# Latent attention on one core: values in three runs of 2, 4 and 4 units in place of five of 2, with a ring of ten places for probabilities

## Chip, core and metric

The kernel runs on one core of a Trainium2 chip. The metric is device time of the whole launch in microseconds (us). Engines: PE is TensorE (PEld its weight loads), DVE is VectorE, ACT is ScalarE, POOL is GpSimd, SP is SyncE.

## What is computed

The input is 4 sequences of 1024 tokens with 128 channels. Six residual blocks follow one another: a mixture of experts, an attention with a polynomial in place of softmax, the mixture again, a feed-forward block, the latent attention, and the feed-forward block again. Only the latent attention (`attn1_phase`) is touched:

```python
Wdkv = x @ latent_w + latent_b                     # keys = values, 36 wide
q = einsum('btc,hcl->bhtl', x, Wd_w) + Wd_b        # 16 heads
scores = einsum('bhtl,bsl->bhts', q, Wdkv) / sqrt(8)
attn = softmax(where(causal, scores, -inf))
y = einsum('bhts,bsl->bhtl', attn, Wdkv)
out = y.transpose(0, 2, 1, 3).reshape(b, t, 576) @ out_w + out_b
```

## The kernel before

The order of the work is written out by hand, per engine, with semaphores. The latent attention goes through 4 sequences ("elements") of 8 pairs of heads. For a pair `m` two things go on at once: its own exponentials and values, and the row maxima of pair `m + 1`, which have to be known before the scores of that pair can be exponentiated.

**Units.** The causal scores of a pair, keys on the partitions, are cut into 10 units (`NU`, L1734). Units 0 to 6 belong to the queries 512 to 1023, units 7 to 9 to the queries 0 to 511. Units 0 to 2 and 7 to 9 lie on the diagonal; POOL zeroes the forbidden part of their probabilities (L1886). Each unit exists for both heads (c = 0, 1). `scores` (L1974) writes one unit and head into one of three PSUM banks; it waits for the exponential three places back (L1972). ACT takes the exponential (L2174) into `probs`, a ring of `RING` = 4 units in SBUF, and waits for the values of the unit `RING` places back (L2172). `values` (L1990) multiplies the two heads' probabilities with V, the heads beside each other in two 64-column halves of the array; every float32 product is two matmul records, and a run of two full units has 8 records, one with a split unit 12. Unit 2 and unit 9 are half as wide (256 columns).

**Maxima.** `scores_max` (L1959) computes the scores of 16 query tiles of the next pair again, queries on the partitions, and DVE reduces each to its row maximum (L2277) and writes it with a short read of its accumulator. Wide tiles (5 to 8 key tiles, 640 to 1024 columns) share one place of two PSUM banks; narrow ones (128 to 512 columns) share a third bank. Each kind has only one buffer: the matmuls of a wide tile wait for DVE to be through with the wide tile before (L1956), and so with the narrow ones. The 16 tiles are dealt into 8 slots, called M0 to M7 here: M0 is one wide tile, M3 is narrow, wide, narrow, and the others are wide, narrow.

**Order on PE** (`pair`, L2012 to L2065), five steps `d` for a pair; S is the scores of one unit and head, V a unit's values:

- d = 0: S 0, S 0, S 1, M0, S 1, then V 8 and V 9 of the pair before
- d = 1: M1, S 2, S 2, S 3, M2, S 3, then V 0, V 1
- d = 2: M3, S 4, S 4, S 5, M4, S 5, then V 2, V 3
- d = 3: M5, S 6, S 6, S 7, M6, S 7, then V 4, V 5
- d = 4: M7, S 8, S 8, S 9, S 9, the transpose of the maxima (L1965), the query projection of pair m + 3 (L1943), then V 6, V 7

The last pair of an element does V 8 and V 9 at its own end. In pair 6 of the first three elements (the opening pair) the latents of the next element are computed in d = 0, and V 8, V 9 and a projection stand ahead of M0, so M0 and M1 follow each other with nothing between. At the start of a pair the first S waits for the maxima to come by DMA into the rows of `qS` (L1971); SP issues those (L1822, L1824) after ACT and DVE have split the transposed maxima in two parts. ACT copies the finished sums out of PSUM (`copy_out`, L2162), the first half after V 6, the second after V 9.

Of the kernel before, what the change touches and what calls it, by code (L numbers as in the profile page):

```python
# [34 lines left out]
def after(n):  # L35

    return n + 1 + LEAD
# [1633 lines left out]
def attn1_phase(nc, t, tag):  # L1671


    with ExitStack() as ctx:
        def sb(name, shape, dt=F32):
            return ctx.enter_context(nc.sbuf_tensor(f"{tag}_{name}", shape, dt))
# [23 lines left out]
        ml = sb("ml", [16, 2, P], F32R)  # L1700
        probs = sb("probs", [P, RING, 2, HALF])
        yT = sb("yT", [P, PAIRS, SEQ])
# [62 lines left out]

        def ring(q, u):

            return (u + 2 * q) % RING

        def o_part(j, rows, n):  # L1770

# [33 lines left out]
        def follows(i, k, more):  # L1805

            return more or i + k < PAIRS

        def projected(i, more):

            return (more or i + 3 < PAIRS) and i != OPENS

        with nc.Block() as block:
# [97 lines left out]
            def _(pe):  # L1911
# [4 lines left out]
                def transpose_x(b):  # L1916
                    for s in range(2):
                        pe.wait_ge(xn_ready, after(b * BT + 4 * s + 3))
                        for j in range(4):
                            last = pe.transpose(m_bank[s][:, j * P:(j + 1) * P], xn[:, 4 * s + j, :], t.ident)  # L1920
                        last.then_inc(xt_ready, 1)

                def latents(b):
                    for s in range(2):
                        pe.wait_ge(xl_ready, after(b * 2 + s))
                        for k, (a, w) in enumerate(PRODUCTS):
                            last = pe.matmul(m_bank[s][0:STACK, :], lat[w][:, :], xT[a][:, s * HALF:(s + 1) * HALF],
                                             start=k == 0, stop=k == 2)
                        last.then_inc(kp_ready, 1)

                def latent_rows(b):
                    pe.wait_ge(xl_ready, after(b * 2 + 1))
                    for j in range(BT):
                        for k, (a, w) in enumerate(PRODUCTS):
                            last = pe.matmul(m_bank[2][:, j * VW:j * VW + LAT], xT[a][:, j * P:(j + 1) * P], lat[w][:, 0:LAT],
                                             start=k == 0, stop=k == 2)
                    last.then_inc(vp_ready, 1)

                def project(p, i):
                    for h, s in enumerate(HALVES):  # L1940
                        pe.wait_ge(qs_ready, after((p - 1) * 2 + h))
                        for k, (a, w) in enumerate(PRODUCTS):
                            last = pe.matmul(m_bank[h][0:2 * LAT, :], wd[w][:, i * 2 * LAT:(i + 1) * 2 * LAT],  # L1943
                                             xT[a][:, s * HALF:(s + 1) * HALF], start=k == 0, stop=k == 2)
                        last.then_inc(qp_ready, 1)

                def scores_max(m, q, n, keys, spare=False):
                    c, j = IN_ORDER[n]
                    before = bank_before(n, spare)
                    if not of_kind(n) and j >= 4:  # L1950
                        pe.wait_ge(q_in[q][0], (m - q) * 48 + 96)
                    elif not of_kind(n):
                        pe.wait_ge(q_in[q][1], (m - q) * 24 + 48)
                        pe.wait_ge(q_first[q], (m - q) * 24 + 48)
                    if before >= 0:
                        pe.wait_ge(mx_ready, after(m * 16 + before))  # L1956
                    for lo in range(0, (j + 1) * P, HALF):
                        hi = min(lo + HALF, (j + 1) * P)
                        last = pe.matmul(max_part(n, lo, hi, spare), qS[q][0:STACK, c, j * P:(j + 1) * P], keys[0:STACK, lo:hi],  # L1959
                                         start=True, stop=True)  # L1960
                    last.then_inc(sm_ready, 1)

                def transpose_max(m, q):
                    pe.wait_ge(mx_ready, after(m * 16 + 15))
                    pe.transpose(o_part(0, 16, P), mx[:, q, :], t.ident).then_inc(mt_ready, 1)  # L1965

                def scores(m, q, u, c):
                    s, pieces = units[u]
                    k = 2 * u + c
                    if u == 0 and c == 0:  # L1970
                        pe.wait_ge(m_in, (m + 1) * 32)  # L1971
                    pe.wait_ge(p_ready, after(m * NE + k - 3 if k >= 3 else (m - 1) * NE + (18, 19, 17)[k]))  # L1972
                    for kt, at_, qc, n, _ in pieces:
                        last = pe.matmul(e_part(k, at_, at_ + n), kS[:, kt * P:(kt + 1) * P],  # L1974
                                         qS[q][:, c, s * HALF + qc:s * HALF + qc + n], start=True, stop=True)
                    last.then_inc(s_ready, 1)
# [35 lines left out]
                def pair(m, i, b, more):  # L2012
                    q = i % 2
                    ahead = follows(i, 1, more)
                    opening = more and i == OPENS + 1
                    keys = kN if i == PAIRS - 1 else kS

                    def maximum(k):
                        if not ahead:
                            return  # L2020
                        if k == 0:
                            if follows(i, 2, more):
                                pe.wait_ge(qs_ready, after((m + 2) * 2 + 1))
                            pe.wait_ge(ml_ready, after(m))
                            if opening:
                                pe.wait_ge(v_ready, after(b + 1))
                        if k == 1 and i == 0:
                            pe.wait_ge(res.xo_ready, after(b * BT - 1))
                        for n in range(FIRST[k], FIRST[k + 1]):
                            scores_max(m + 1, 1 - q, n, keys)  # L2030

                    for d in range(STEPS):
                        if d == 0 and opening:
                            latents(b + 1)
                        if d >= 1:
                            maximum(2 * d - 1)
                        for u, c in ((2 * d, 0), (2 * d, 1), (2 * d + 1, 0)):
                            scores(m, q, u, c)
                        if d == 0 and opening:
                            pe.wait_ge(ml_ready, after(m))  # L2040
                            latent_rows(b + 1)
                        if d < STEPS - 1 and not (d == 0 and opening):
                            maximum(2 * d)
                        scores(m, q, 2 * d + 1, 1)
                        if d == STEPS - 1:
                            if ahead:
                                transpose_max(m + 1, 1 - q)
                            if more and i == OPENS:
                                transpose_x(b + 1)
                            if projected(i, more):  # L2050
                                project(m + 3, (i + 3) % PAIRS)
                        if d == 0:
                            if i > 0:
                                for u in (NU - 2, NU - 1):
                                    values(m - 1, 1 - q, u)
                            if opening:
                                pe.wait_ge(ks_ready, after(b * 2 + 3))
                                project(m + 2, 0)
                                maximum(0)
                        else:  # L2060
                            for u in (2 * d - 2, 2 * d - 1):
                                values(m, q, u)
                    if i == PAIRS - 1:
                        for u in (NU - 2, NU - 1):
                            values(m, q, u)  # L2065

                def finish(b, more):
# [39 lines left out]
                    if more:  # L2107
                        pe.wait_ge(kc_ready, after(b + 1))

                pipeline(pe, start, pair, finish)  # L2110

            @block.scalar
            def _(act):
# [50 lines left out]
                def pair(m, i, b, more):  # L2164
# [3 lines left out]
                    def exponent(u, c):  # L2168
                        k = 2 * u + c
                        act.wait_ge(s_ready, after(m * NE + k))  # L2170
                        if c == 0:
                            act.wait_ge(pv_ready, after(m * NU + u - RING))  # L2172
                        n = 256 if len(units[u][1]) == 1 and units[u][1][0][3] == 256 else HALF
# [147 lines left out]
        sem.end()  # L2321


RING = 4
OPENS = PAIRS - 3


# [127 lines left out]
```

## Time and profile before

| | us |
|---|---|
| median of 3 runs | 3007.7 |
| lowest and highest | 3005.54, 3011.52 |
| the profiled execution, its own time | 3009.96 |
| its span | 3008.2 |
| of it, the pairs and element ends of the latent attention | 2042 to 2893 |

[...]

### The profile page before, as it was taken

How to read it: one execution, taken by the hardware profiler on the slowest of the kernel's cores; microseconds unless marked ns; L12 is line 12 of the kernel's file. 1: busy time of each engine (PE TensorE's matmuls, PEld its weight loads, DVE VectorE, ACT ScalarE, POOL GpSimd, SP SyncE). 2: the span in 40 equal slices, each digit the busy share in tenths (PEclk: the TensorE clock that was granted, in tenths of full speed). 3: DMA queues.
4: the chain of work that ended last, by engine and by line, in shares of the span. 5: the costliest groups of instructions: out<-in, count | busy, mean ns of one | idle time of the engine just before them, and what ended most of it. 6: DMA issues, size and time to landing. Idle time of an engine off the chain costs nothing. (4 is left out here: it accounts for less than half of the span.)

```text
span 3008.2 us, 53420 instructions
## 1 busy us (share of the span) xinstructions
PE 2717.3 (90%) x15208; PEld 1878.1 (62%) x15208; DVE 1908.3 (63%) x5011; ACT 1136.8 (38%) x2101; POOL 924.1 (31%) x1235
## 2 busy tenths in 40 slices
PE   6999999968888888789999999778998998998989
PEld 5888888845555555468888888434455455455454
DVE  6777777746665666477777777445555555555542
ACT  3111111116666667521111111234544544544544
POOL 3222233216666666542222222001111211211200
PEclk9999999968898898889999999888999999999999
DMA  4000000000000000110000000001111111111100
GB/s 138 0 0 0 0 0 0 0 1 2 2 3 3 3 3 3 36 67 0 0 0 0 0 0 1 1 21 28 43 31 28 43 30 28 43 29 31 43 2 28
DMA packets 31963, 51.87 MB, mean 17 GB/s; under 512 B 8178, under 2 KB 14066, under 8 KB 31732
## 3 DMA queue, kind: packets, MB, share of 16 engines
q1 hardware_dynamic: 27124, 41.88, 4.6%
q0 software_dynamic: 4608, 7.09, 0.9%
q8 instruction: 124, 2.03, 0.3%
q14 instruction: 107, 0.88, 0.1%
HBM read 17.93 MB, written 2.10 MB: 7 GB/s over the span
## 5 line engine op out<-in xcount | busy, mean ns | idle before, releaser
L640 DVE SCALAR_TENSOR_TENSOR moe_acc<-moe_ps,moe_comb,moe_acc 128x512 f32<-128x512 f32 x896 | 660.9, 744 | 154.5 <-PE moe_ps L346 151.5
L2277 DVE CUSTOM_DVE_ANT_0 attn_masked<-attn_psm,attn_causal 128x1024 f32<-128x1024 f32 (+1 forms) x504 | 363.2, 757 | 260.4 <-PE attn_psm L1959 259.7
L2174 ACT ACTIVATE attn_probs<-attn_pse 128x512 f32<-128x512 f32 (+1 forms) x640 | 313.6, 556 | 342.4 <-PE attn_pse L1974 339.8
L377 PE MATMUL moe_ps<-moe_Wd,moe_ih 128*128 128x512 f32 x1024 | 344.1, 418 | 4.6 <-DVE moe_Wd L563 4.6
L346 PE MATMUL moe_ps<-moe_Wg,moe_xh 128*128 128x512 f32 x1024 | 328.9, 403 | 16.9 <-DVE moe_Wg L563 16.9
L346 PE MATMUL moe_ps<-moe_Wu,moe_xh 128*128 128x512 f32 x1024 | 334.1, 408 | 2.7 <-POOL moe_Wu L501 2.7
L1886 POOL TENSOR_SCALAR_AFFINE_SELECT attn_probs<-attn_probs 128x256 f32<-128x256 f32 (+1 forms) x192 | 95.1, 496 | 711.9 <-ACT attn_probs L2174 711.8
L1990 PE MATMUL attn_psy<-attn_probs,attn_V 128*64 128x512 f32 (+3 forms) x1536 | 291.4, 510 | 0.0
L511 POOL TENSOR_SCALAR moe_part<-consts,moe_pick,moe_prob 128x8 f32<-128x8 f32 x256 | 97.9, 400 | 626.9 <-ACT moe_prob L434 626.9
L1959 PE MATMUL attn_psm<-attn_kS,attn_qS 108*128 108x512 f32 (+3 forms) x672 | 197.8, 395 | 49.9 <-DVE attn_mx L2277 43.9
L1145 POOL TENSOR_TENSOR attn_R<-attn_R 128x1024 f32<-128x1024 f32 (+1 forms) x128 | 213.9, 1681 | 92.5 <-DVE attn_R L1511 91.7
L346 PEld LDWEIGHTS moe_ps<-moe_Wg,moe_xh 128*128 128x128 f32 x1024 | 195.2, 192 | 65.7 <-issue 20.8
L1974 PE MATMUL attn_pse<-attn_qS,attn_kS 110*128 110x512 f32 (+3 forms) x768 | 207.5, 366 | 23.3 <-ACT attn_probs L2174 10.3
L346 PEld LDWEIGHTS moe_ps<-moe_Wu,moe_xh 128*128 128x128 f32 x1024 | 191.3, 192 | 47.0 <-issue 5.4
L1959 PEld LDWEIGHTS attn_psm<-attn_kS,attn_qS 108*128 108x128 f32 x672 | 112.5, 195 | 168.0 <-DVE attn_mx L2277 147.4
L433 ACT ACTIVATE moe_prob<-moe_gap 128x2 f32<-128x2 f32 x64 | 13.0, 203 | 519.4 <-DVE moe_gap L631 519.4
L377 PEld LDWEIGHTS moe_ps<-moe_Wd,moe_ih 128*128 128x128 f32 x1024 | 182.8, 193 | 41.0 <-issue 4.8
L346 PE MATMUL moe_ps<-moe_Wg,moe_xl 128*128 128x512 f32 x512 | 205.2, 401 | 0.0
L346 PE MATMUL moe_ps<-moe_Wu,moe_xl 128*128 128x512 f32 x512 | 204.8, 400 | 0.0
L377 PE MATMUL moe_ps<-moe_Wd,moe_il 128*128 128x512 f32 x512 | 203.6, 398 | 0.0
L1511 DVE TENSOR_SCALAR attn_R<-attn_e 128x1024 f32<-128x1024 f32 (+1 forms) x128 | 139.2, 1087 | 92.9 <-PE attn_e L1210 87.1
L1990 PEld LDWEIGHTS attn_psy<-attn_probs,attn_V 128*64 128x64 f32 x1536 | 97.0, 140 | 134.7 <-issue 122.9
(233 smaller groups left out, 4686.9 us busy)
## 6 DMA issues: line engine op xcount, KB each, us to landing
attn_qS<-attn_qH SPq DMA_DIRECT2D x192, 72.0 KB
attn_qS<-attn_qL SPq DMA_DIRECT2D x96, 72.0 KB
attn_qS<-attn_qH POOLq DMA_DIRECT2D x64, 72.0 KB, 2.0
moe_stageg<-in_w_gate SPq DMA_DIRECT2D x8, 512.0 KB, 7.2
moe_stageu<-in_w_up SPq DMA_DIRECT2D x8, 512.0 KB, 7.4
moe_stageg<-in_w_down SPq DMA_DIRECT2D x8, 512.0 KB, 4.0
attn_qS<-attn_qL POOLq DMA_DIRECT2D x32, 72.0 KB, 2.5
out<-X SPq DMA_DIRECT2D x8, 256.0 KB, 2.4
```

The costliest lines, as they stand in the source:

```text
L346: last = pe.matmul(expert_bank[j % 4][:, :], a[q][:, :], w[b][:, cols], start=k == 0, stop=k == 2)
L377: last = pe.matmul(y_bank[h][:, :], a[q][:, rows], W[2][b][:, cols], start=c == 0 and k == 0, stop=c == KC - 1 and k == 2)
L511: ins = pool.tensor_scalar(part[:, q, r, k, :], t.iota8, pick[:, q, r, k:k + 1], prob[:, q, r, k:k + 1], ALU.is_equal, ALU.mult)
L640: dve.scalar_tensor_tensor(acc[:, q, r, :], expert_bank[j % 4][:, :], comb[:, q, r, e:e + 1], acc[:, q, r, :], ALU.mult, ALU.add).then_inc ...
L1145: pool.tensor_tensor(r, r, r, ALU.mult).then_inc(sq01_ready, 1)
L1511: dve.tensor_scalar(R[:, r, 0:2, HALF - n:HALF], e01[u % 2][:, :, HALF - n:HALF], LIFT, -HALF_LIFT, ALU.max, ALU.add).then_inc(read01, 1)
L1886: pool.affine_select(some, some, [[0, 2], [0, (hi - lo) // P], [1, P]], ALU.is_ge, nothing, base=0, channel_multiplier=-1).then_inc(tri_re ...
L1959: last = pe.matmul(max_part(n, lo, hi, spare), qS[q][0:STACK, c, j * P:(j + 1) * P], keys[0:STACK, lo:hi], start=True, stop=True)
L1974: last = pe.matmul(e_part(k, at_, at_ + n), kS[:, kt * P:(kt + 1) * P], qS[q][:, c, s * HALF + qc:s * HALF + qc + n], start=True, stop=True)
L1990: last = pe.matmul(y_bank[h][VW * c:VW * (c + 1), qc:qc + n], V[:, kt, :], probs[:, ring(q, u), c, at_:at_ + n], start=first and k == 0, s ...
L2174: act.activation(probs[:, ring(q, u), c, HALF - n:HALF], e_part(k, HALF - n, HALF), ACT.Exp, scale=SCORE_SCALE).then_inc(p_ready, 1)
L2277: dve.tensor_tensor_reduce(masked[:, 0 if j >= 4 else 1, 0:n], max_part(k, 0, n, spare), causal[:, SEQ - n:SEQ], 1.0, NEG, ALU.add, ALU.ma ...
```

## The change

The values are issued in steps 2 and 4 only, four units each; the pair's units 8 and 9 stay in step 0 of the next pair. The ring has ten places, one for each unit of a pair, and a unit's place is its number. `probs` grows from 16 to 40 KB in each partition. No instruction is added or removed: the order on PE, the buffers and the number waited for in L2172 change.

```diff
         def ring(q, u):
 
-            return (u + 2 * q) % RING
+            return u
...
                                 pe.wait_ge(ks_ready, after(b * 2 + 3))
                                 project(m + 2, 0)
                                 maximum(0)
-                        else:
-                            for u in (2 * d - 2, 2 * d - 1):
+                        elif d in (2, 4):
+                            for u in range(2 * d - 4, 2 * d):
                                 values(m, q, u)
...
-RING = 4
+RING = 10
```

## Rows read from the trace of the kernel before

**Rows 1.** The page: the span, and busy time and idle time of three groups

```profile
span 3008.2 us, 53420 instructions
L2277 DVE CUSTOM_DVE_ANT_0 attn_masked<-attn_psm,attn_causal 128x1024 f32<-128x1024 f32 (+1 forms) x504 | 363.2, 757 | 260.4 <-PE attn_psm L1959 259.7
L2174 ACT ACTIVATE attn_probs<-attn_pse 128x512 f32<-128x512 f32 (+1 forms) x640 | 313.6, 556 | 342.4 <-PE attn_pse L1974 339.8
L1990 PE MATMUL attn_psy<-attn_probs,attn_V 128*64 128x512 f32 (+3 forms) x1536 | 291.4, 510 | 0.0
```

**Rows 2.** Windows: stretch, length, PE, PEld, DVE, ACT, POOL busy, granted clock, DMA

```profile
2042.00:2893.00 851.00, 769.52 (x3916) 439.39 (x3917) 473.37 (x1289) 417.81 (x852) 144.91 (x288) 0.97 0.12 33
2137.37:2160.35 22.98, 21.18 (x103) 11.21 (x103) 13.27 (x35) 12.37 (x25) 4.49 (x9) 1.00 0.14 38
600.00:1200.00 600.00, 499.31 (x4528) 326.33 (x4530) 361.33 (x585) 364.28 (x460) 353.53 (x205) 0.85 0.01 2
```

**Rows 3.** Timeline of PE, one steady pair: start, length, operation, idle before

```profile
2137.39 0.97 PE L1974 MATMUL attn_pse<-attn_qS,attn_kS 110*128 110x512 f32 x4 [0.29 <-DMA attn_qS<-attn_ml]
...
2142.40 1.11 PE L1959 MATMUL attn_psm<-attn_kS,attn_qS 108*128 108x512 f32 x3 [0.54 <-DVE attn_mx L2277]
2143.35 0.40 PE L1974 MATMUL attn_pse<-attn_qS,attn_kS 110*128 110x512 f32 x1
2143.68 1.94 PE L1990 MATMUL attn_psy<-attn_probs,attn_V 128*64 128x512 f32 x12
2145.55 0.80 PE L1959 MATMUL attn_psm<-attn_kS,attn_qS 108*128 108x384 f32 x3
2146.84 0.44 PE L1959 MATMUL attn_psm<-attn_kS,attn_qS 108*128 108x384 f32 x1 [0.49 <-DVE attn_mx L2277]
...
2148.74 1.51 PE L1990 MATMUL attn_psy<-attn_probs,attn_V 128*64 128x256 f32 x8
2150.18 0.72 PE L1959 MATMUL attn_psm<-attn_kS,attn_qS 108*128 108x512 f32 x3
...
2152.80 1.94 PE L1990 MATMUL attn_psy<-attn_probs,attn_V 128*64 128x512 f32 x8
2154.67 0.67 PE L1959 MATMUL attn_psm<-attn_kS,attn_qS 108*128 108x512 f32 x3
...
2158.21 1.94 PE L1990 MATMUL attn_psy<-attn_probs,attn_V 128*64 128x512 f32 x8
2160.37 0.50 PE L1974 MATMUL attn_pse<-attn_qS,attn_kS 110*128 110x512 f32 x1 [0.23 <-DMA attn_qS<-attn_ml]
```

**Rows 4.** Timeline of DVE in the same pair: reads that free a buffer

```profile
2142.26 0.08 DVE L2277 DVE_READ_ACCUMULATOR2_ANT attn_mx<- 128x1 f32 x1
...
2145.11 0.08 DVE L2277 DVE_READ_ACCUMULATOR2_ANT attn_mx<- 128x1 f32 x1
...
2153.76 0.08 DVE L2277 DVE_READ_ACCUMULATOR2_ANT attn_mx<- 128x1 f32 x1
```

**Rows 5.** Timeline of PE in the first opening pair: M0, then M1

```profile
2193.22 0.71 PE L1959 MATMUL attn_psm<-attn_kS,attn_qS 108*128 108x512 f32 x2 [1.88 <-DVE attn_qL L2253]
2195.50 0.84 PE L1959 MATMUL attn_psm<-attn_kS,attn_qS 108*128 108x512 f32 x3 [1.57 <-DVE attn_mx L2277]
```

**Rows 6.** Windows around the clock's fall in two opening pairs

```profile
2192.90:2196.30 3.40, 1.51 (x7) 1.02 (x7) 1.32 (x3) 0.00 (x0) 0.00 (x0) 1.00 0.00 0
2196.30:2203.10 6.80, 6.52 (x21) 2.78 (x19) 3.42 (x8) 1.80 (x4) 0.42 (x1) 0.51 0.01 2
2185.46:2218.42 32.96, 28.02 (x131) 15.43 (x132) 16.18 (x40) 13.91 (x28) 4.49 (x9) 0.90 0.09 24
2409.20:2443.74 34.54, 29.65 (x131) 16.32 (x132) 16.20 (x40) 13.94 (x28) 4.49 (x9) 0.85 0.09 23
```

**Rows 7.** Timeline of PE, last element: start of its pairs 6 and 7, end

```profile
2852.21 0.96 PE L1974 MATMUL attn_pse<-attn_qS,attn_kS 110*128 110x512 f32 x4 [1.17 <-DMA attn_qS<-attn_ml]
...
2875.77 0.96 PE L1974 MATMUL attn_pse<-attn_qS,attn_kS 110*128 110x512 f32 x4 [2.12 <-DMA attn_qS<-attn_ml]
...
2879.95 0.50 PE L1974 MATMUL attn_pse<-attn_qS,attn_kS 110*128 110x512 f32 x1 [0.39 <-ACT attn_probs L2174]
```

## The prediction

> **What bounds the kernel now.** I read the page first, for the share of the latent attention in the whole: its pairs run from 2042 to 2893 us, 851 of the span's 3008.2 us [rows 1, 2]. Only these can change. The windows of that stretch come next: PE is busy 769.5 of 851 us, DVE 473.4, ACT 417.8, POOL 144.9 [rows 2]. PE is the engine with no time to spare, and its queue is in order, so any wait in it that is not there now lengthens the stage. The groups tell what the others do: DVE sat idle 260 us for maxima that PE had not computed yet, ACT 342 us for scores [rows 1]. Neither is a bound by its sum; each is a chain that PE must feed and come back to. The timeline of one steady pair, 22.98 us from its first score to the next pair's, shows where PE pays for that [rows 2, 3]: it waits 0.29 us for the DMA of the maxima, and 0.54 and 0.49 us for DVE to free a buffer. The starts of M3 and M7 (2145.55 and 2154.67) have no wait [rows 3]. The question is whether that is so because DVE is fast enough or because the values ahead of them last long enough. DVE's timeline answers it: the narrow maximum that M3 must wait for is read out at 2145.11, 0.08 us long, so at 2145.19; the wide one that M7 must wait for at 2153.84 [rows 4]. From such a read to the first matmul takes 0.06 us (2142.26 + 0.08, then 2142.40) [rows 3, 4]. So M3 could start at 2145.25 and M7 at 2153.90, only 0.30 and 0.77 us before they do. The values ahead of them, 1.87 us each (2143.68 to 2145.55, 2152.80 to 2154.67), hide a DVE latency; they are not in its way.
>
> **The change, part by part.**
>
> *1. What the fewer runs save.* V 2 and V 3, one and a half full units, take 1.44 us from start to start (2148.74 to 2150.18), V 4 and V 5, two full ones, 1.87 [rows 3]. Half a unit is thus 0.43 us, four halves 1.72, and 0.15 us a run is left for going into and out of the 64-column halves. Four runs go into two: 0.15 us twice in a pair. [...] Over 32 pairs this is 64 x 0.15 = 9.6 us less.
>
> *2. V 0 and V 1 leave step 1.* After the last score of step 1 PE comes to M3 at 2143.68 in place of 2145.55, and M3's first tile, narrow, waits for M2's narrow tile until 2145.25. All that follows up to V starts 0.30 us earlier, not 1.87. The moved units add 1.87 - 0.15 = 1.72 us to the run in step 2. Sum: 1.72 - 0.30 = +1.42 us a pair. Everything ahead of it in the pair is unchanged: the wait of 0.54 us at M2 stays, and so does the wait of 0.49 us inside M3, which is a wait of one of M3's tiles for another.
>
> *3. V 4 and V 5 leave step 3.* PE comes to M7 at 2152.80 and waits for M6's wide tile until 2153.90; the chain moves 0.77 us forward, and 1.72 us are added at the end of step 4: +0.95 us. There the longer run covers something: the first score of the next pair waits for the maxima's DMA, 0.29 us in [rows 3], and the run of four units outlasts it. Net +0.66 us in a steady pair. M1, M2, M4, M5 and M6 get no new wait: M5 follows a longer run than before, and M1 still has V 8 and V 9 ahead.
>
> *4. Other engines.* The ring took no part: an exponential four units on came after the values it waits for, and with ten places it needs the unit of the pair before, long done; cost nothing, gain nothing. ACT's copy of the first half waits for V 6, which is still followed by V 7 and then by the next pair's scores, so its 0.6 us lies where it lay. The projection's work of ACT and DVE gets a longer cover. POOL's masking of unit 7 has one run more of time. SP's and POOL's query DMAs go by scores and keep their order. The 8 scores of steps 1 and 2 come in a row, but with DVE's stall among them they come no faster than ACT takes them.
>
> *5. Sum without the clock.* A steady pair: 1.42 + 0.66 = +2.08 us. There are 23: pairs 0 to 4 and the opening pair 6 of three elements, and pairs 0 to 4 of the last. The three pairs 5 that transpose x in place of the projection have a longer DMA wait to cover; between 2.08 and the 0.65 of a pair whose wait takes the whole added run I take 1.4 each. The three last pairs of elements with a successor have no DMA wait at their end: 1.42 + 0.95 = 2.37 each. In the last element the idle times before pairs 6 and 7 are 1.17 and 2.12 us [rows 7], because no projection stands ahead; the longer run (1.72 us) fits nearly or wholly into them: 1.1 and 0.65 us for its pairs 5 and 6. Its pair 7 has no maxima and waits for ACT (0.39 us, [rows 7], and three more like it); four of them are some 1.1 us, and I take -0.9, since ACT keeps its own pace. 23 x 2.08 = 47.8; 3 x 1.4 = 4.2; 3 x 2.37 = 7.1; 47.8 + 4.2 + 7.1 + 1.1 + 0.65 - 0.9 = **+60 us** (the 9.6 us of part 1 are in it). Bounds: the two stalls could be 0.3 us shorter each if DVE gets to its work sooner (+42), or as much longer (+78).
>
> *6. The clock.* In the steady pair the granted clock is 1.00, full speed [rows 2]. In the opening pair M0 and M1 follow each other without values between; PE waits 1.57 us for DVE there [rows 5]. [...] The price of low time comes from two opening pairs with the same work: 32.96 us at a mean clock of 0.90 and 34.54 us at 0.85 [rows 6], that is 6.6 and 10.4 us at half clock, so 1.58 us for 3.8, 0.42 for each. A fall of 6.8 us then costs 2.9 us. With one in nine of ten of the 31 pairs that compute maxima: 31 x 0.9 x 2.9 = **+81 us**. From below: none, 0 us. From above: the polynomial attention, with PE busy 499 of 600 us, runs at 0.85 [rows 2], so 30% of its time is at half clock; at 30% of 25 us, 7.5 us a pair, and at most half of it lost, 3.75 x 31 = 116 us. I take the opening pair's price because its stall is of the same engines and the same size.
>
> [...]
>
> **Total:** 3009.96 + 60 + 81 = 3151 for an execution like the profiled one; that one lay 2.3 us above the median, which is within the spread of the runs (6 us). I forecast 3150.
>
> **The rivals.**
>
> *A. The clock stays up.* The stalls come as worked out, but PE's short runs between them are enough. For: the opening pair has a second wait, 1.88 us for qL, just before [rows 5], and both together may be what it took. [...] 3010 + 60 = 3070 us. [...] Chance 0.17.
>
> *B. Two falls in a pair.* M7's stall (1.1 us of waiting) makes the clock fall again, and the projection and V 4 to V 7 run at half speed. For: 0.85 as the mean of another stage [rows 2]. Against: more scores stand around M7 than around M3. 31 x (2 x 2.9) = 180: 3010 + 60 + 180 = 3250 us. Chance 0.09.
>
> *C. Faster: DVE is not late.* Place: M3 and M7. If DVE's reads came early enough for PE to find both buffers free, each pair would lose nothing, gain 2 x 0.15 us of runs and the DMA wait of 0.29: 0.59 x 31 = 18 us, 2992 us. It decides from the point at which the reads come 1.5 us (M3) and 1.0 us (M7) sooner after the matmuls than in [rows 4]. For: DVE is busy only 13.27 of 22.98 us [rows 2]. Against: its reads in this very order are at 2145.19 and 2153.84, and nothing in the change moves them ahead. Chance 0.04.
>
> *D. No difference.* The runs of values are not what PE's queue does in fact, because scores wait for ACT in any case and the sum of stalls is only shared out anew: 3008 +- 6. ACT's idle 342 us for PE speaks against it [rows 1]. Chance 0.02.
>
> **How the numbers follow.** The forecast has 0.68: own range 3110 to 3200 (60 give or take 18, and the clock from 58, two pairs in three, to 116). The range given reaches down over rival A, to 3062, and up to 3220, between the forecast and B; it leaves out B, C, D and A's lower part. About 0.2% of the time, 6 us, is what a measurement here can tell from no change. Faster by more than that: rival C, 0.04. Within it: 0.02. Slower: 0.94.
>
> **What would show it.** In the profile after, the timeline of a steady pair should show M3 with an idle time of about 1.5 us before it, released by attn_mx L2277, M7 with 1.0 us, one run of V 0 to V 3 of 3.2 us and one of V 4 to V 7 of 3.6 us at full clock, and no DMA wait ahead of the first score. The pair should take 25.1 us where the clock is 1.00 and 28 us where it falls; the windows of the stage should show a clock of about 0.85 to 0.9 in place of 0.97. The wait list should show PE's wait for attn_mx rise from a few tens of us to over 100. I am wrong if M3 starts with no wait, if the pair stays near 23 us, or if the clock stays 1.00 through such pairs; the last alone would leave rival A.

## The result and the profile after

The changed kernel takes 3177.8 us (median of 4 runs, 3170.2 to 3183.2) against 3008.4 for the kernel before; the ratio is 1.056, 95% interval 1.0539 to 1.0580. It is 169 us slower, 5.6%. The forecast was 3150 us with a range up to 3220. The instruction counts of all engines are those of before; the whole difference lies in the latent attention, whose pairs and element ends now fill 1020 us in place of 851.

The page of the kernel after has its span, the slices of the granted clock and two groups. The span, from the first instruction in the trace to the last, is 3177.6 us; the same execution took 3179.3 by its own time, 1.7 us more:

```profile
span 3177.6 us, 53420 instructions
...
PEclk9999999968888898799999999688878888788889
...
L2277 DVE CUSTOM_DVE_ANT_0 attn_masked<-attn_psm,attn_causal 128x1024 f32<-128x1024 f32 (+1 forms) x504 | 364.4, 757 | 376.2 <-PE attn_psm L1959 374.5
L2174 ACT ACTIVATE attn_probs<-attn_pse 128x512 f32<-128x512 f32 (+1 forms) x640 | 316.4, 555 | 407.9 <-PE attn_pse L1974 405.3
```

DVE and ACT do what they did, in the same time for one instruction, and sit idle for PE longer: DVE 376 us in place of 260, ACT 408 in place of 342 [rows 1]. In the 15 last slices, where the latent attention is, the clock has eights, two sevens and a six. The granted clock is TensorE's, and 1.00 is the highest level in the traces. The windows of the stage say how much that is, for the kernel after and for one of its steady pairs (columns as in [rows 2]):

```profile
2040.00:3060.00 1020.00, 881.65 (x3895) 519.28 (x3896) 475.43 (x1288) 423.91 (x851) 144.45 (x288) 0.83 0.10 28
2099.02:2128.49 29.47, 25.50 (x105) 14.01 (x104) 13.32 (x35) 12.61 (x25) 4.49 (x9) 0.83 0.12 32
```

The mean clock of the stage is 0.83, it was 0.97, and the pair takes 29.5 us where one took 23.0 [rows 2]. The trace's records of the clock have two levels, 1 and 0.5, and nothing between; the windows of low time below read 0.50 and 0.51. With these a mean of 0.83 over 1020 us is 347 us at half clock (0.17 x 2 x 1020); before it was 51 us (0.03 x 2 x 851). PE's waits for `attn_mx` at L1959 add up to 120.7 us in this stage; before they were 47.6. The timeline of PE in that pair shows where the waits and the low time lie:

```profile
2104.27 1.11 PE L1959 MATMUL attn_psm<-attn_kS,attn_qS 108*128 108x512 f32 x3 [0.54 <-DVE attn_mx L2277]
2105.21 0.40 PE L1974 MATMUL attn_pse<-attn_qS,attn_kS 110*128 110x512 f32 x1
2107.12 0.79 PE L1959 MATMUL attn_psm<-attn_kS,attn_qS 108*128 108x384 f32 x3 [1.51 <-DVE attn_mx L2277]
2108.40 0.50 PE L1959 MATMUL attn_psm<-attn_kS,attn_qS 108*128 108x384 f32 x1 [0.49 <-DVE attn_mx L2277]
2108.70 1.48 PE L1974 MATMUL attn_pse<-attn_qS,attn_kS 110*128 110x512 f32 x3
...
2111.50 3.49 PE L1990 MATMUL attn_psy<-attn_probs,attn_V 128*64 128x512 f32 x20
...
2118.64 0.93 PE L1959 MATMUL attn_psm<-attn_kS,attn_qS 108*128 108x512 f32 x3 [1.03 <-DVE attn_mx L2277]
2119.36 2.08 PE L1974 MATMUL attn_pse<-attn_qS,attn_kS 110*128 110x384 f32 x6
2121.24 0.41 PE L1965 MATMUL attn_psm<-consts,attn_mx 128*16 128x128 f32 x1
2121.31 2.91 PE L1943 MATMUL attn_psm<-attn_xT,attn_wd 128*72 128x512 f32 x6
2124.15 4.41 PE L1990 MATMUL attn_psy<-attn_probs,attn_V 128*64 128x512 f32 x16
2128.49 0.96 PE L1974 MATMUL attn_pse<-attn_qS,attn_kS 110*128 110x512 f32 x4
```

The reader sees both waits that had been hidden: 1.51 us before M3 and 1.03 us before M7, where there was none [rows 3]. Behind each the matmuls are long: the three scores in M3's wake take 1.48 us for 0.87 before, the projection 2.91 (1.64 in the kernel before, from 2156.64, at clock 1.00), and the last run of values 4.41. The first score of the next pair has no wait for its DMA any more, 0.29 before [rows 3].

Windows show the low time itself, two stretches of it in this pair and two in the next, whose M3 starts at 2136.33 and whose M7 starts at 2148.81:

```profile
2108.60:2112.10 3.50, 3.50 (x10) 2.38 (x11) 2.05 (x5) 2.07 (x4) 0.00 (x0) 0.51 0.00 0
2118.90:2125.80 6.90, 6.90 (x20) 3.90 (x21) 2.82 (x7) 3.26 (x7) 2.59 (x5) 0.51 0.35 94
2135.90:2142.70 6.80, 6.17 (x15) 3.81 (x17) 3.83 (x12) 2.17 (x4) 0.00 (x0) 0.50 0.00 0
2149.60:2153.00 3.40, 3.40 (x12) 2.26 (x11) 1.32 (x5) 2.08 (x6) 1.70 (x4) 0.50 0.28 76
```

Here a short stretch at half clock behind M3 goes with a long one behind M7, and in the next pair, where the first begins just before M3, it is the other way round. Of the 31 pairs that compute maxima, 26 have low time at M3 and all 31 at M7; before, none has any at either place.

### The profile page after: what moved, and what is told of

The parts are those of the page before. It is cut to its first block and busy times, and to the rows that moved or that the text cites. A ratio compares the mean times of both kernels' runs of the same rounds, so it can differ in the third digit from the quotient of the medians.

```text
span 3177.6 us, 53420 instructions
## 1 busy us (share of the span) xinstructions
PE 2830.3 (89%) x15208; PEld 1957.6 (62%) x15208; DVE 1911.2 (60%) x5011; ACT 1143.7 (36%) x2101; POOL 922.4 (29%) x1235
## 3 DMA queue, kind: packets, MB, share of 16 engines
q8 instruction: 125, 2.05, 0.3%
## 5 line engine op out<-in xcount | busy, mean ns | idle before, releaser
L2277 DVE CUSTOM_DVE_ANT_0 attn_masked<-attn_psm,attn_causal 128x1024 f32<-128x1024 f32 (+1 forms) x504 | 364.4, 757 | 376.2 <-PE attn_psm L1959 374.5
L1959 PE MATMUL attn_psm<-attn_kS,attn_qS 108*128 108x512 f32 (+3 forms) x672 | 222.0, 437 | 115.4 <-DVE attn_mx L2277 109.3
L1990 PE MATMUL attn_psy<-attn_probs,attn_V 128*64 128x512 f32 (+3 forms) x1536 | 303.0, 541 | 0.0
L1959 PEld LDWEIGHTS attn_psm<-attn_kS,attn_qS 108*128 108x128 f32 x672 | 134.1, 225 | 228.9 <-DVE attn_mx L2277 182.8
L1974 PE MATMUL attn_pse<-attn_qS,attn_kS 110*128 110x512 f32 (+3 forms) x768 | 251.5, 434 | 7.5 <-issue 5.5
L1990 PEld LDWEIGHTS attn_psy<-attn_probs,attn_V 128*64 128x64 f32 x1536 | 106.7, 152 | 163.0 <-issue 152.2
L1974 PEld LDWEIGHTS attn_pse<-attn_qS,attn_kS 110*128 110x128 f32 x768 | 164.7, 237 | 54.3 <-issue 28.5
```

What stands on the lines that cost most here:

```text
L1990: last = pe.matmul(y_bank[h][VW * c:VW * (c + 1), qc:qc + n], V[:, kt, :], probs[:, ring(q, u), c, at_:at_ + n], start=first and k == 0, s ...
L2277: dve.tensor_tensor_reduce(masked[:, 0 if j >= 4 else 1, 0:n], max_part(k, 0, n, spare), causal[:, SEQ - n:SEQ], 1.0, NEG, ALU.add, ALU.ma ...
```

## The experiments

Three theories stood against each other. The first is that of the prediction: the moved values uncover two DVE waits in each pair (worth 60 us), and the clock falls in them (worth the rest). The second: the 170 us are waits alone, and the low clock only fills time that would be idle. The third: the long runs of values or the ring cost by themselves.

**The ring alone** (label ring_only): the kernel before with `RING = 10` and `return u`, the runs left as five.

> The ring of ten places alone, values in five runs as before. Theory (two DVE stalls in a pair, and a clock that falls in them; the ring takes no part): within 0.2% of before, 3008 us, clock 0.97 in the stage. Rival (the ring's places or the wait on the values matter): a difference of over 10 us either way.

Measured 3008.5 us, ratio 1.0004 (0.9991 to 1.0017). Its stage reads 851.00 us at a mean clock of 0.97, like before. The ring takes no part.

**Each pair of runs joined by itself.** First V 0 and V 1 moved alone (label join_first), then V 4 and V 5 alone (join_second), both written as edits of the changed kernel:

```diff
-                        elif d in (2, 4):
-                            for u in range(2 * d - 4, 2 * d):
+                        elif d > 1:
+                            for u in range(0 if d == 2 else 2 * d - 2, 2 * d):
```

```diff
-                        elif d in (2, 4):
-                            for u in range(2 * d - 4, 2 * d):
+                        elif d != 3:
+                            for u in range(4 if d == 4 else 2 * d - 2, 2 * d):
```

> Only V 0 and V 1 are moved from step 1 to step 2; V 4, V 5 and V 6, V 7 stay in steps 3 and 4. Theory: the stall before M3 alone, +1.42 us in each of 31 pairs (+44 us), and one fall of the clock in each pair at or behind it, of 3.4 to 6.8 us of low time, +1.2 to +2.5 us (+37 to +78 us): 3089 to 3130 us; M3 idle 1.5 us, M7 idle nothing. Rival 1 (the clock falls only because the two places come together): 3052 us with a clock of 0.97. Rival 2 (no cost of its own by the clock, the 170 us are waits): about half of 170, 3093, but with the idle time of PE accounting for all of it.

> Only V 4 and V 5 are moved from step 3 to step 4; V 0, V 1 and V 2, V 3 stay in steps 1 and 2. Theory: the stall before M7 alone, +0.66 us a pair (+20 us), and its fall of the clock of 6.8 us of low time in most pairs, +2 to +2.9 us (+62 to +90 us): 3090 to 3118 us, so that the clock costs several times what the stall does. Rival 1 (falls need both places): 3028 us, clock 0.97. With the kernel that moves only V 0 and V 1 the two differences should add up to about 170 us if the places act each by itself.

V 0 and V 1 moved alone: 3127.2 us, ratio 1.0395 (1.0377 to 1.0414), +118 us. V 4 and V 5 alone: 3059.2 us, 1.0162 (1.0145 to 1.0179), +50 us. The sum, 168 us, is the change's 169. The first is within what was expected; the second is 31 us below the expected range. Two stretches of the second kernel, each as long as one pair, and its stage tell why:

```profile
2070.30:2096.60 26.30, 24.01 (x105) 12.85 (x104) 13.33 (x35) 12.46 (x26) 4.50 (x9) 0.87 0.13 35
2313.00:2336.60 23.60, 21.00 (x105) 11.27 (x104) 13.32 (x35) 12.36 (x26) 4.51 (x9) 1.00 0.15 39
2044.00:2935.00 891.00, 789.54 (x3854) 456.58 (x3855) 474.36 (x1289) 411.59 (x836) 143.41 (x284) 0.92 0.12 32
```

Both pairs have the wait of 1.03 us before M7. Where the clock stays at 1.00 the pair takes 23.6 us, 0.6 to 0.7 more than before, as forecast for M7's stall. Where it falls for 6.8 us (13% of 26.3, twice) the pair takes 26.3. I had expected such a fall in most pairs. The trace has one at M7 in 21 of the 31 pairs, and in 15 of these it lasts only half as long, 3.4 us. With M3's stall of 1.5 us alone the clock falls in 25 of 31 pairs, in 23 of them for 6.8 us.

**Useless matmuls in the waits.** If the clock is the cost, PE should be faster with more to do. Ahead of M3 and M7 these were added to the changed kernel (label fill_both), with `FILL = {2: 6, 4: 4}`; they write a bank that the next scores overwrite.

```diff
+                        if ahead and d in FILL:
+                            s = units[2 * d][0]
+                            pe.wait_ge(p_ready, after(m * NE + 4 * d - 3))
+                            for _ in range(FILL[d]):
+                                pe.matmul(e_part(4 * d, 0, HALF), kS[:, 0:P], qS[q][:, 0, s * HALF:(s + 1) * HALF],
+                                          start=True, stop=True)
                         if d >= 1:
                             maximum(2 * d - 1)
```

> The changed kernel with matmuls added that compute nothing that is used: 6 of 512 columns ahead of M3 and 4 ahead of M7 in each pair, into the bank that the next scores overwrite. They take 1.4 and 0.94 us at full clock, just the 1.5 and 1.0 us in which PE waits there. Theory (the clock makes about 110 of the 170 us): the clock stays up, near 0.97 in the stage, and the time falls to 3070 us, give or take 15, although PE does more. Rival (waits and order make the 170 us, the low clock only fills idle time): 3178 us or more, as the added matmuls cost nothing at best.

Measured 3075.5 us, ratio to before 1.0219 (1.0199 to 1.0239): 102 us less than the changed kernel, with 310 more matmuls (10 in each of 31 pairs). PE's timeline in one pair of it, and the windows of its stage (L2039 are the added matmuls; the added lines make L2277 into L2283):

```profile
2101.59 0.96 PE L1974 MATMUL attn_pse<-attn_qS,attn_kS 110*128 110x512 f32 x4
...
2106.83 1.11 PE L1959 MATMUL attn_psm<-attn_kS,attn_qS 108*128 108x512 f32 x3 [0.54 <-DVE attn_mx L2283]
2107.77 0.40 PE L1974 MATMUL attn_pse<-attn_qS,attn_kS 110*128 110x512 f32 x1
2108.01 1.54 PE L2039 MATMUL attn_pse<-attn_qS,attn_kS 110*128 110x512 f32 x6
2109.67 0.79 PE L1959 MATMUL attn_psm<-attn_kS,attn_qS 108*128 108x384 f32 x3
...
2112.85 3.23 PE L1990 MATMUL attn_psy<-attn_probs,attn_V 128*64 128x512 f32 x20
2116.01 0.73 PE L1959 MATMUL attn_psm<-attn_kS,attn_qS 108*128 108x512 f32 x3
...
2118.53 1.09 PE L2039 MATMUL attn_pse<-attn_qS,attn_kS 110*128 110x512 f32 x4
2119.72 0.67 PE L1959 MATMUL attn_psm<-attn_kS,attn_qS 108*128 108x512 f32 x3
...
2123.25 3.65 PE L1990 MATMUL attn_psy<-attn_probs,attn_V 128*64 128x512 f32 x16
2126.84 0.96 PE L1974 MATMUL attn_pse<-attn_qS,attn_kS 110*128 110x512 f32 x4
```

```profile
2050.00:2960.00 910.00, 829.34 (x4215) 501.35 (x4216) 473.97 (x1289) 417.12 (x852) 145.46 (x288) 0.97 0.11 31
```

M3 starts 2.84 us after M2, in the changed kernel it was 2.85: the added matmuls took only time in which PE waited for DVE. The clock of the stage is back at 0.97. The pair, from its first score at 2101.59 to the next one's at 2126.84, takes 25.25 us. In none of the 31 pairs does the clock fall at M3 or M7. This sets the two parts apart: +67 us are the stalls (60 had been worked out), with whatever the added matmuls cost by themselves, and 102 us are the clock. The second theory, by which added work could not help, is out.

**One wait filled at a time.**

> The changed kernel with the 6 added matmuls ahead of M3 alone; M7's wait is left empty. Theory (each stall makes its own fall): the falls at M3 go, those at M7 stay. 3178 less the clock's part of the first place. That part is, from the kernel that moved only V 0 and V 1 (+118 us, of which 44 are the stall), 74 us: 3104 us. Rival (one fall drags the other with it, so that without the first there is no second): about 3075 us, as with both filled.

> The changed kernel with the 4 added matmuls ahead of M7 alone; the wait before M3 is left empty. With both filled it took 3075 us, with M3's alone 3093. If each place makes its own fall, the falls behind M3 stay as where only V 0 and V 1 were moved (6.8 us of low time in a pair, 3127 us), and M7's stall of 0.66 us a pair comes on top, 20 us: 3147 us, 10 either way. If the fall at M7 happens only behind one at M3, the result is the same. If most of the low time is of M7's making, it comes out near 3100.

With `FILL = {2: 6}` (label fill_first) 3093.4 us, ratio 1.0285 (1.0269 to 1.0300), stage clock 0.94; with `FILL = {4: 4}` (fill_second) 3125.0 us, 1.0396 (1.0378 to 1.0414), stage clock 0.88. Both came out below what was expected, by 11 and 22 us. With M3 filled the clock falls at M7 in 20 of 31 pairs, in 19 of them for the short 3.4 us, and M7's wait costs 18 us of clock there (3093.4 less 3075.5). With M7 filled it falls at M3 in 28 pairs, mostly for 6.8 us, as expected; the stage's clock is 0.88 all the same, where it was 0.86 with V 0 and V 1 moved alone, and the reason was not looked for.

Filling M3's wait gives back 84 us, M7's 53, both 102. The two add up to 137, so by these runs some 35 us of clock cost (some 30 by the ratios) is there only where both waits are. The kernels with one pair of runs joined say otherwise: less the stalls of 44 and 20 us as worked out, their clock costs are 74 and 30 us, which add up to 104, about the 102 of both. So whether the two waits cost more together than each by itself is not settled. What the traces do show is where the low time goes: with both waits empty M7's falls are more and longer than with M7's wait alone (31 pairs, 13 of them with the long fall, against 21 with 6, or 20 with 1), and M3's are shorter (15 of 26 are short, against 1 of 25). Why is only open to argument.

**DVE's work cut in both kernels** (labels cut_before and cut_after). The maxima are reduced over the last 128 columns of each tile only, which leaves out the rest of the row maximum, so that DVE is hardly ever late.

```diff
-                    dve.tensor_tensor_reduce(masked[:, 0 if j >= 4 else 1, 0:n], max_part(k, 0, n, spare), causal[:, SEQ - n:SEQ],
+                    dve.tensor_tensor_reduce(masked[:, 0 if j >= 4 else 1, 0:P], max_part(k, n - P, n, spare), causal[:, SEQ - P:SEQ],
```

> The kernel before, with DVE reducing only the last 128 columns of each tile of maxima: it leaves out the rest of the row maximum. A wide tile then takes DVE 0.29 us in place of 0.8 to 1.2, and PE's waits for its buffers should go. This is the base for the same cut in the changed kernel. Theory and rival alike: 0.5 to 1.3 us less in each of 31 pairs, 2970 to 2995 us, clock 0.97 or above.

> The changed kernel with the same cut: DVE reduces only the last 128 columns of each tile, the rest of the row maximum is left out. Theory (the change loses only by DVE's lateness at M3 and M7, and the clock that falls in those waits): with DVE no longer late it is as fast as the cut kernel before or faster, by 2 x 0.15 us of runs and a hidden DMA wait of 0.29 us in a pair, 0 to 18 us. Rival (the long runs of values and the bunched scores cost by themselves, through ACT or the clock): slower than the cut kernel before by over 20 us.

The cut kernel before took 2944.7 us (ratio to before 0.9791, 0.9775 to 0.9806), the cut changed kernel 2948.7 (0.9807, 0.9791 to 0.9823). The intervals overlap: without DVE's lateness the change is worth nothing that can be measured, where it had cost 169 us. The third theory, that long runs cost by themselves, falls. That the change gains nothing either is in its timeline; this is the cut changed kernel:

```profile
2105.60 0.79 PE L1959 MATMUL attn_psm<-attn_kS,attn_qS 108*128 108x384 f32 x3 [0.44 <-DVE attn_mx L2277]
...
2114.07 0.67 PE L1959 MATMUL attn_psm<-attn_kS,attn_qS 108*128 108x512 f32 x3 [0.19 <-DVE attn_mx L2277]
```

Even a reduction of 128 columns, 0.29 us on DVE, leaves waits of 0.44 and 0.19 us at M3 and M7: what is left of the way from PE to DVE and back. They eat the 0.6 us that fewer runs and the hidden DMA were to save: this pair takes 21.57 us (2099.62 to 2121.19), the same pair of the cut kernel before 21.37 (2101.11 to 2122.48). The clock of both stages is 0.97. The base was 25 us faster than I had expected, in part because a steady pair became shorter by 1.6 us (21.37 for the 22.98 of [rows 2]) and not by 1.3 at most; the rest lies outside the steady pairs.

**Can the waits that are left in the kernel before be used?** Three small edits of the kernel before were run, and one kernel with two of them. The first (label deal_before) deals the tiles of maxima otherwise:

```diff
-        MAXIMA = [WIDE[0:1], (WIDE[1], NARROW[0]), (WIDE[2], NARROW[1]), (NARROW[2], WIDE[3], NARROW[3]),
-                  (WIDE[4], NARROW[4]), (WIDE[5], NARROW[5]), (WIDE[6], NARROW[6]), (WIDE[7], NARROW[7])]
+        MAXIMA = [WIDE[0:1], (WIDE[1], NARROW[0]), (WIDE[2], NARROW[1]), (WIDE[3], NARROW[2]),
+                  (WIDE[4], NARROW[3]), (WIDE[5], NARROW[4]), (WIDE[6], NARROW[5]), (NARROW[6], WIDE[7], NARROW[7])]
```

> The kernel before with the 16 tiles of maxima dealt otherwise: M3 is one wide and one narrow tile in place of narrow, wide, narrow; every later slot has the narrow tile that was one slot ahead, and M7 is narrow, wide, narrow with the two of 128 columns. Theory (PE waits for DVE where two tiles of one kind follow each other closely; 0.49 us inside M3): that wait goes, M7's small tiles cost nothing new: 0.3 to 0.5 us less in 31 pairs, 10 to 15 us, 2993 to 2999 us. Rival (DVE is the bound over steps 1 and 2, so the wait moves to M4): 3008 us, no difference beyond 0.2%.

3019.0 us, ratio 1.0040 (1.0026 to 1.0054): slower by 11 us. One pair of it, from M3 to the transpose of the maxima:

```profile
2099.11 0.79 PE L1959 MATMUL attn_psm<-attn_kS,attn_qS 108*128 108x512 f32 x3
...
2100.97 0.92 PE L1959 MATMUL attn_psm<-attn_kS,attn_qS 108*128 108x512 f32 x3 [0.37 <-DVE attn_mx L2277]
...
2107.99 0.67 PE L1959 MATMUL attn_psm<-attn_kS,attn_qS 108*128 108x128 f32 x3
2108.89 0.33 PE L1959 MATMUL attn_psm<-attn_kS,attn_qS 108*128 108x128 f32 x1 [0.23 <-DVE attn_mx L2277]
...
2110.49 0.27 PE L1965 MATMUL attn_psm<-consts,attn_mx 128*16 128x128 f32 x1
```

In the steady pair of [rows 3] the transpose is here:

```profile
2156.61 0.28 PE L1965 MATMUL attn_psm<-consts,attn_mx 128*16 128x128 f32 x1
```

The wait of 0.49 us inside M3 went, and one of 0.37 came at M4, as the rival said. Up to M7 there is still something gained: 8.88 us from M3 to M7, 9.12 before. It is lost at M7, which neither theory nor rival had: with three tiles, the last of which waits 0.23 us for DVE, it is 2.50 us from M7 to the transpose in place of 1.94. Net this is 0.3 us a pair, 10 us in 31 pairs. Here the 0.49 us taken out at one tile came back as 0.37 at the next, and the third tile in M7's slot cost a wait of its own, 0.23.

The other two use the slack that the prediction had read, 0.30 us at M3 and 0.77 us at M7. V 5 held back (label hold_v5, with `RING = 10` and `return u`):

```diff
-                            for u in (2 * d - 2, 2 * d - 1):
+                            for u in ((0, 1), (2, 3), (4,), (5, 6, 7))[d - 1]:
```

One score ahead of M2 (early_s3):

```diff
+                        if d == 1:
+                            scores(m, q, 3, 1)
                         if d < STEPS - 1 and not (d == 0 and opening):
                             maximum(2 * d)
-                        scores(m, q, 2 * d + 1, 1)
+                        if d != 1:
+                            scores(m, q, 2 * d + 1, 1)
```

> The kernel before with one unit moved, and the ring of ten: V 5 goes from step 3 to step 4, runs of 2, 2, 2, 1 and 3. M7's slack over DVE is 0.77 us, a unit is 0.86 us, so M7 waits for 0.1 us only, and the longer last run covers the 0.29 us wait for the maxima's DMA. Theory: 0.2 us less a pair, more in the last element, where that wait is 1.2 and 2.1 us: 3000 to 3004 us, clock 0.97. Rival (any unit moved from M7 costs): 3015 or more.

> The kernel before with one score moved: the second head of unit 3 is computed ahead of M2 in place of behind it, in the 0.54 us in which PE waits there for DVE. ACT frees its bank about 0.2 us after PE comes to it, so M2 starts no later and V 0, V 1 start 0.24 to 0.33 us sooner. M3 can follow by 0.30 us at most, by its slack over DVE. Theory: 0.24 us less a pair, 7 us: 3001 us. Rival (M3's slack is less in most pairs, or ACT's chain is delayed): 3008 us or more.

> Both small moves at once, V 5 into step 4 and the second head of unit 3 ahead of M2. They touch different places of the pair, so theory: the sum of the two, 0.4 us a pair, 12 to 15 us less than before, 2993 to 2997 us.

V 5 held back: 3005.2 us, 0.9993 (0.9982 to 1.0004), no difference that can be told from zero, where 4 to 8 us less had been expected. The early score: 3000.0 us, 0.9971 (0.9958 to 0.9983), as expected. Both: 2991.1 us, 0.9953 (0.9937 to 0.9969), 14 us less by the ratio, as expected; the median lies 2 us below the range. This kernel is faster than both of the study, by 0.5% against the kernel before. In its timeline the pair, from score to score, is 22.53 us long (2129.19 to 2151.72) where the pair of the same number took 22.98, M2 has no wait, M7 none, and the last run of three units covers the DMA:

```profile
2133.86 0.49 PE L1974 MATMUL attn_pse<-attn_qS,attn_kS 110*128 110x512 f32 x1 [0.20 <-ACT attn_probs L2177]
2134.20 1.11 PE L1959 MATMUL attn_psm<-attn_kS,attn_qS 108*128 108x512 f32 x3
...
2145.44 0.67 PE L1959 MATMUL attn_psm<-attn_kS,attn_qS 108*128 108x512 f32 x3
...
2148.99 2.79 PE L1990 MATMUL attn_psy<-attn_probs,attn_V 128*64 128x512 f32 x12
2151.72 0.97 PE L1974 MATMUL attn_pse<-attn_qS,attn_kS 110*128 110x512 f32 x4
```

## Why the prediction held, and where it was off

**What bounds the kernel, and parts 2 and 3.** The reading that the values before M3 and M7 hide a DVE latency, with slacks of 0.30 and 0.77 us, is confirmed. From M2 to M3 it was 3.15 us and is 2.85 now, from M6 to M7 it was 2.82 (2151.85 to 2154.67) and is 2.05 (2116.59 to 2118.64): just these 0.30 and 0.77 us earlier. PE's timeline keeps the order of `pair`: nothing that stands behind M3 or M7 starts in the 1.51 and 1.03 us of waiting. The forecast named idle times of about 1.5 and 1.0 us, the trace has 1.51 and 1.03. The pair at full clock was to take 2.08 us more; with the waits filled it takes 25.25 us, where the pair of the same number took 23.19 before, 2.06 more.

**Part 5, the sum without the clock.** +60 us worked out, +67 us measured (3075.5 to 3008.4), of which a few may belong to the added matmuls. One term of the sum is added up wrongly: pair 5 of the last element comes to 1.42 + 0.95 - 1.17 = 1.20 us, not 1.1. Nothing hangs on it.

**Part 1, fewer runs.** The 0.15 us a run was only a small term. The runs of four units, forecast at 3.2 and 3.6 us, take 3.16 and 3.59 us from start to start at full clock (2112.85 to 2116.01 and 2123.25 to 2126.84 with both waits filled), which is 3.5 and 4 units of 0.86 us and one 0.15 each. A run's time is taken from start to start because the records of two runs overlap in the trace: 2112.85 and 3.23 us make 2116.08, and the next run starts at 2116.01. That the 0.15 us comes from going into and out of the 64-column halves was not tested by itself.

**Part 4, the ring and the other engines.** Ratio 1.0004 for the ring alone; no wait of another engine took DVE's place.

**Part 6, the clock.** This is the term that was mis-sized. It was taken as one fall of 6.8 us in nine of ten pairs, 190 us of low time, 81 us of cost; measured are 296 us more of low time than before, and 102 us of cost. The nine in ten was the author's estimate; the trace has 26 in 31 at M3. That there would be a fall in a steady pair at all was judged from the opening pair [rows 6]: 0.51 for 6.80 us, behind 3.40 us in which PE is busy 1.51. In the 3.4 us up to 2145.25, the earliest start of M3, PE has 1.35 us of work beside the values that were to move, from 2142.40 to 2143.75 [rows 3]. In the kernel after PE is busy 1.40 us in the 3.40 ahead of the steady pair's first fall, and 2.14 in the 3.40 ahead of its second, more than the opening pair's 1.51:

```profile
2105.20:2108.60 3.40, 1.40 (x6) 0.67 (x5) 2.66 (x7) 0.60 (x1) 0.00 (x0) 1.00 0.00 0
2115.50:2118.90 3.40, 2.14 (x9) 1.30 (x9) 2.49 (x8) 2.17 (x4) 0.42 (x1) 1.00 0.16 43
```

The forecast counted a fall at M3 alone, and left M7's stall without one. The runs show falls at both: in the changed kernel 26 pairs have one at M3 and all 31 at M7, mostly one of 3.4 and one of 6.8 us, about 10 us a pair. That is rival B's mechanism, two falls, but not its size, as one of the two is mostly half as long as it assumed. So the stage's clock is 0.83, below the forecast's 0.85 to 0.9, and the pair takes 29.5 us where 28 had been forecast.

The price had been 0.42 us for each low microsecond, from two opening pairs. In the steady pair above it is 0.41 (4.2 us, 29.47 against 25.25, for 3.4 + 6.8 us); over the stage it is less, 102 us for 296, 0.34; why it is less there is open. At 0.42 the 296 us would have cost 124. The two errors, too little low time and too high a price, partly cancel, and that the total of 3150 us came so near to 3178 owes something to this luck. A bound stated in the part held the measured cost: 116 us from the 0.85 of the polynomial attention [rows 2], against 102 measured. The stage's clock goes from 0.97 to 0.83 with no idle time of PE in that steady pair above 1.51 us.

**Rival A** (the clock stays up, 3070 us) did not happen, but the kernel with both waits filled is close to what it describes, 3075 us. **Rival C** was to be decided by whether DVE's reads could come 1.5 and 1.0 us earlier. With DVE cut to 128 columns they come earlier, though waits of 0.44 and 0.19 us are left, and even then there is no gain. **Rival D**, no difference, is out by 169 us.

## What to carry to other kernels

A run of work that needs no other engine is not only work: where it stands between a producer's two uses of one buffer, it hides the round trip. Here 1.87 us of values hid 1.51 us of waiting at M3, and as much hid 1.03 at M7. Before it is moved, read from the other engine's timeline when the buffer comes free, and compare that with when the work now ends; the difference, 0.30 and 0.77 us here, is all that was gained by moving it, and the rest came back as a wait. This kernel paid for such waits again through TensorE's clock, 102 us on top of 67, and matmuls that compute nothing were a quick test of how much of the loss that was.

## What was not expected of the hardware

Useless work made the kernel faster: 10 matmuls of 512 columns in each of 31 pairs, 102 us less. And the length of a wait alone does not tell what the clock does: with V 4 and V 5 moved alone, a wait of 1.03 us let the clock fall in some pairs and not in others whose instructions are the same (26.3 us at a mean clock of 0.87, 23.6 us at 1.00).
